# Two mixture-of-experts layers around two attentions: second weights resident in SBUF, one layer's weights parked in DRAM, unused tiles left out

## What is computed

```python
x = x + 0.5 * L0_ffn(norm(x))    # 24 experts, D_FF 512, top 2 of 24
x = x + L0_attn(norm(x))         # linear attention, 16 "heads", softplus features
x = x + 0.5 * L0_ffn(norm(x))
x = x + 0.5 * L1_ffn(norm(x))    # 8 experts, H 256, top 2 of 8, and a shared expert
x = x + L1_attn(norm(x))         # causal softmax attention with rotary embedding
x = x + 0.5 * L1_ffn(norm(x))
```

## Time and profile before

| | us |
|---|---|
| median of 3 runs | 1047.45 (1044.62 to 1049.02) |
| span of the profiled execution (first to last instruction) | 1043.2 |
| TensorE busy / weight loads, beside it | 905.4 / 789.0 |
| VectorE, ScalarE, GpSimd busy | 569.7, 484.6, 497.2 |
| data moved | 200.19 MB |

### The profile page before, as it was taken

How to read it: one execution, slowest core, us unless ns; L and a number is a source line. 1 busy time by engine, 2 the same in 40 slices (tenths; PEclk the granted TensorE clock), 3 DMA queues, 4 the chain that set the end, 5 groups by cost and what they waited for, 6 DMA issues and landing times.

```text
span 1043.2 us, 26677 instructions
## 1 busy us (share of the span) xinstructions
PE 905.4 (87%) x8696; PEld 789.0 (76%) x8696; DVE 569.7 (55%) x2226; ACT 484.6 (46%) x814; POOL 497.2 (48%) x519
## 2 busy tenths in 40 slices
PE   4757999998999799999999998996899999998670
PEld 2327899976889777899888898883688867888570
DVE  7897500066785065785058400588883888872112
ACT  3333544448634257734345444352528455654320
POOL 0551560271027571035372743577744657277655
PEclk9886999999999899999999999898999999999985
DMA  9765999973578783488895899944658456669982
GB/s 306 242 205 156 300 308 242 237 203 95 123 191 231 187 212 104 118 208 234 218 254 146 209 274 226 230 129 130 153 141 189 124 115 165 142 155 247 258 196 75
DMA packets 278655, 200.19 MB, mean 192 GB/s; under 512 B 146112, under 2 KB 233536, under 8 KB 278400
## 3 DMA queue, kind: packets, MB, share of 16 engines
q1 hardware_dynamic: 262144, 164.90, 63.1%
q0 software_dynamic: 16384, 33.59, 11.2%
HBM read 115.56 MB, written 55.57 MB: 164 GB/s over the span
## 4 chain that ended last, share of the span: by engine, by line
PE 58%; DVE 20%; DMA 8%; issue 5%; ACT 4%; POOL 4%; SPq 1%; DVEq 0%; POOLq 0%; ACTq 0%
PE bank L1425 20%; PE bank L1403 5%; PE bank L1405 5%; PE bank L1404 5%; DMA turned<-rows 4%; PE bank L1291 4%; POOL got L2123 3%; PE bank L1244 3%; DMA got<-y_l,slot_index 3%; PE bank L1263 2%; PE bank L1220 2%; PE bank L1253 2%; PE bank L1422 2%; DVE xn L1708 2%; PE bank L1301 2%
## 5 line engine op out<-in xcount | busy, mean ns | idle before, releaser
L1425 PE MATMUL bank<-second,hid 128*128 128x128 f32 x2560 | 369.7, 287 | 0.0
L2123 POOL DMA_INDIRECT got<-y_l,slot_index x256 | 244.7, 956 | 236.4 <-DMA y_l<-y 114.3
L1425 PEld LDWEIGHTS bank<-second,hid 128*128 128x128 f32 x2560 | 324.7, 195 | 4.7 <-issue 3.0
L2103 POOL DMA_INDIRECT rows<-rows_sent,slot_index x192 | 187.8, 978 | 282.2 <-issue 167.7
L1575 ACT ACTIVATE hid<-bank 128x512 f32<-128x512 f32 x320 | 189.7, 597 | 280.4 <-PE bank L1405 266.0
L1403 PE MATMUL bank<-turned,blocks_l 128*128 128x128 f16 x1280 | 239.7, 222 | 41.1 <-DMA turned<-rows 31.2
L1921 DVE SCALAR_TENSOR_TENSOR x_res<-got,share,x_res 128x128 f32<-128x128 f32 x256 | 77.4, 348 | 319.5 <-DMA got<-y_l,slot_index 312.9
L1405 PE MATMUL bank<-turned,blocks_l 128*128 128x128 f16 x1280 | 239.8, 223 | 0.0
L1404 PE MATMUL bank<-turned,blocks_l 128*128 128x128 f16 x1280 | 239.1, 222 | 0.0
L1403 PEld LDWEIGHTS bank<-turned,blocks_l 128*128 x1280 | 127.6, 100 | 55.4 <-issue 52.7
L1404 PEld LDWEIGHTS bank<-turned,blocks_l 128*128 x1280 | 127.1, 99 | 8.9 <-issue 5.9
(11 more groups left out here) (208 smaller groups left out, 1215.6 us busy)
## 6 DMA issues: line engine op xcount, KB each, us to landing
second<-in_w_dram SPq DMA_DIRECT2D x243, 256.0 KB, 5.3
y_l<-y SPq DMA_DIRECT2D x104, 256.0 KB
second<-in_w_dram SPq DMA_DIRECT2D x192, 128.0 KB
got<-y_l,slot_index POOLq DMA_INDIRECT x256
rows<-set SPq DMA_DIRECT2D x1, 3584.0 KB, 14.9
rows<-set SPq DMA_DIRECT2D x7, 512.0 KB, 6.4
rows<-rows_sent,slot_index POOLq DMA_INDIRECT x192
hid<-in_w_dram SPq DMA_DIRECT2D x9, 256.0 KB, 5.2
```

Source lines behind the costliest of these rows:

```text
L1425: m = t.do.matmul(out, hid[:, at], second[:, at], start=False, stop=(c == C - 1))
L2103: d = g.do.indirect_dma_start(rows_dram[s], at, rows[:, 2 * D * i:2 * D * i + 2 * D], None)
L2123: d = g.do.indirect_dma_start(got_mem[slot][:, col:col + D], None, y_dram[layer][s][layer.team(ev.i)], at)
```

## The change

- `w2` of all experts is loaded once, fp32, into `blocks` beside the halves of `w1` (a block is now `2 * hidden + 4` words). `bring` and its buffers, registers and DMAs go. `l2` reads the block at the tile's address.
- The 128 columns of each selector become one column, which a matmul reads with step 0 (`spread`); `select_cut`, `first_select` and their loads go.
- Room: layer 1's `blocks` are filled, stored to `blocks_dram` (`park`), used as two of the three sets of the linear attention, and loaded back (`unpark`) when all linear products are made. Round 2 has two sets of two buffers. Weights and tables of the causal attention are loaded into layer 0's `blocks` after its last experts (`load_late`, `load_last`).
- Row buffers: 6 in place of 8, taken for a batch before its norm and given back after its scatter. `hid`: 4 in place of 3. Raw buffers: 8 for layer 0, 4 for layer 1. Layer 0's routing has one scratch (in `route_wide`).
- `l2` is planned behind the third following `l1`, not the second. Layer 1's first matrices are split after layer 0's, and layer 0's experts no longer wait for them.
- Tiles beyond the bound are neither computed nor stored: 55 and 23.
- The planner's durations and the rank table change.

```diff
-        self.units = self.tiles // self.unit
+        self.bound, self.unit = bound, SEQ // hidden
+        self.units = -(-bound // self.unit)
-        self.block = hidden + P // 2
+        self.block = 2 * hidden + 4
+    def filled(self, unit):
+        return min(self.unit, self.bound - unit % self.units * self.unit)
...
-RAW_BUFFERS = 10
+GOT_BUFFERS, HID_BUFFERS, ROW_BUFFERS = 4, 4, 6
+RAW_BUFFERS = [HID_BUFFERS + GOT_BUFFERS, GOT_BUFFERS]
+FIRSTS_AHEAD = 3
+PARKED_SETS = (0, 1)
+MID_SETS, MID_BUFFERS = 2, 2
...
-        "scatter": [[(GP, 1.27 * TOP_K * tokens, 2.2)]], "gather": [[(GP, 1.27 * TOP_K * BT, 2.4)]], "add": [[(VE, 2.4, 0.1)]],
+        "scatter": [[(GP, 1.1 * TOP_K * tokens, 2.2)]], "gather": [[(GP, 1.1 * TOP_K * BT, 2.4)]], "add": [[(VE, 2.8, 0.1)]],
-        "bring": [[(SY, 0.45 * unit + 0.08, 0.0), (DMA, 0.9, 2.0)]],
+        "fetch": [[(SY, 1.3, 0.0), (DMA, 1.75, 2.0)]],
-        "l1": [[(PE, 0.75, 0.22), (SC, 0.62, 0.16)]], "l2": [[(PE, 1.04 if unit == 1 else 1.09, 0.22)]]
+        "l1": [[(PE, 0.68, 0.22), (SC, 0.58, 0.16)]], "l2": [[(PE, 1.03 if unit == 1 else 1.17, 0.22)]]
... # Plan.prepare: behind layer 0's loads and splits
+        yield Await(["halved"])
+        for n, ev in enumerate(later):
+            self.spawn(first(ev) if ev.kind.startswith("w1") else second(ev), (0, 2, len(parts) + n))
+        yield Await([split_of(ev) for ev in W1_PARTS[1]] + W2_PARTS[1])
+        yield from load("park")
+        for n in PARKED_SETS:
+            self.open_set(n)
+        yield from load("load_weights")
+        yield Await(["zeroed"])
+        self.open_set(START_SET)
+        yield Await(["linears"])
+        self.grow(self.mid_sets, MID_SETS, Ev("linears", 0, 0, 0))
+        yield from load("unpark")
... # Plan.gate, experts
+        yield Take(self.rows, [Ev("turn_g", s, p, b)], 1)
-            yield Await([("l1", s, p, min(unit + 2, units[-1]))])
+            yield Await([("l1", s, p, min(unit + FIRSTS_AHEAD, units[-1]))])
... # rank_on
-    rank = (rank[0] + EARLIER.get((engine, ev.kind), 0),) + rank[1:]
-    if engine == PE:
-        return (expert, ev.kind == "l1") + rank
-    return (not expert, False) + rank
+    shift = EARLIER.get((engine, ev.kind), FIRST if expert and engine != PE else 0)
+    rank = (rank[0] + shift,) + rank[1:]
+    return (expert, ev.kind == "l1") + rank if engine == PE else rank
... # layer1, layer2
-                for j in range(layer.unit):
+                for j in range(layer.filled(ev.i)):
-                    select = block_parts(block_for(ev, j), H)[2]
-                    t.do.matmul(out, select, bcol("b2_0" if layer is L0 else "b2_1"), start=True, stop=False)
-                    for c in range(C):
-                        at = slice(j * H + c * P, j * H + c * P + P)
-                        m = t.do.matmul(out, hid[:, at], second[:, at], start=False, stop=(c == C - 1))
+                    _, _, second, select = block_parts(block_for(ev, j), H)
+                    t.do.matmul(out, spread(select), bcol("b2_0" if layer is L0 else "b2_1"), start=True, stop=False)
+                    for c, at in enumerate(spans(C)):
+                        m = t.do.matmul(out, hid[:, j * H + c * P:j * H + c * P + P], second[:, at], start=False, stop=(c == C - 1))
... # SyncE
+            def park_blocks(ev):
+                y.wait_ge(*w1_low.after_all(w1_splits[1]))
+                y.wait_ge(second_loaded[1], 16 * SECOND_LOADS)
+                y.wait_ge(*selects_made.after(SELECTS))
+                y.do.dma_start(blocks_dram, blocks[L1][:, :]).then_inc(block_parked.sem, 16)
+            def bring_blocks(ev):
+                y.wait_ge(block_parked, 16)
+                for s, outs in enumerate(every_out):
+                    y.wait_ge(*attn_made[s].after_all(outs))
+                y.do.dma_start(blocks[L1][:, :], blocks_dram).then_inc(block_back.sem, 16)
+            def load_second(ev, layer, source):
+                some = slice(ev.i * layer.E // SECOND_LOADS, (ev.i + 1) * layer.E // SECOND_LOADS)
+                dst = blocks[layer].rearrange("p (e c) -> p e c", e=layer.E)[:, some, layer.H:2 * layer.H]
+                y.do.dma_start(dst, source[some].rearrange("e p h -> p e h")).then_inc(second_loaded[int(ev.kind[3:])].sem, 16)
-            def bring_second(ev, expert):
...
-                for j in range(layer.unit):
-                    dst = second_mem[slot][:, j * H:(j + 1) * H].unsqueeze(1)
-                    y.do.dma_start(dst, w2[:, bass.ds(expert[ev.i * layer.unit + j], 1)]).then_inc(second_landed[slot].sem, 16)
```

More of the change, by code:

```diff
@@ L73 @@
 L1 = Layer("l1", 8, 256, 2)
+assert all(l.teams == 1 or l.units * l.unit == l.tiles for l in (L0, L1))
 MAX_TILES = max(l.tiles * l.teams for l in (L0, L1))
@@ L285, in __init__ @@
         self.banks = Pool(8)
-        self.xn, self.xt, self.sets, self.got, self.norms = Pool(2), Pool(2), Pool(EARLY_SETS), Pool(4), Pool(2)
-        for held in (BIAS_SET, ZERO_SET):
-            self.sets.free.remove((held, None))
-        self.late_sets, self.raw = Pool(0), Pool(RAW_BUFFERS)
-        self.turned, self.second, self.hid, self.y = Pool(4), Pool(7), Pool(3), Pool(2)
-        self.tensor = Pool(1)
+        self.xn, self.xt, self.sets, self.got, self.norms = Pool(2), Pool(2), Pool(EARLY_SETS), Pool(GOT_BUFFERS), Pool(2)
+        self.sets.free = []
+        self.mid_sets, self.late_sets, self.raw = Pool(0), Pool(0), [Pool(n) for n in RAW_BUFFERS]
+        self.turned, self.hid, self.y, self.rows = Pool(4), Pool(HID_BUFFERS), Pool(2), Pool(ROW_BUFFERS)
+        self.tensor, self.scratch = Pool(1), Pool(1)
+        self.linears, self.routes = STREAMS * SB, STREAMS * sum(PARTS[p] for p in range(ROUNDS) if LAYER[p] is L0)
         self.now, self.count, self.events, self.done, self.waiting, self.kept = 0.0, 0, [], set(), [], STREAMS
@@ L466, in prepare @@
             self.spawn(load("load_x", 0, b), rank)
-        for kind in ("load_half", "load_bias", "load_cut"):
+        for kind in ("load_half", "load_bias"):
             self.spawn(load(kind), rank)
+        self.spawn(selects(), rank)
+        self.spawn(ready(), rank)
         yield Sleep(4.0)
-        parts = [part(n) for n in range(len(W1_PARTS))]
-        for n, steps in enumerate(parts):
-            self.spawn(steps, (0, 2, n))
+        parts, later = W1_PARTS[0] + W2_PARTS[0], W1_PARTS[1] + W2_PARTS[1]
+        for n, ev in enumerate(parts):
+            self.spawn(first(ev) if ev.kind.startswith("w1") else second(ev), (0, 2, n))
             if n == 3:
@@ L484, in prepare, with late @@
         self.spawn(self.zeros(), rank)
[L485 to L492 removed]
+        yield Await(["halved"])
[11 more added lines that the diff above has]
+        yield from load("unpark")
+    def late(self):
+        for kind in ("load_late", "load_last"):
+            yield from self.stage(kind, 0, 0, 0)
+            self.mark(kind)
     def zeros(self):
@@ L591, in linear, with out @@
         yield from self.stage("la_moved", s, p, b)
-        yield from self.stage("la_out", s, p, b, {PE: lambda: self.give(self.sets, user)})
+        def out():
+            self.linears -= 1
+            if self.linears:
+                self.give(self.sets, user)
+            else:
+                self.mark("linears")
+        yield from self.stage("la_out", s, p, b, {PE: out})
     def causal(self, s, p, b):
+        yield Await(["load_late", "load_last"])
         yield from self.normed("a", s, p, b)
@@ L642, in ranked @@
             if layer is L0:
-                self.give(self.sets, user)
+                self.routes -= 1
+                self.give(self.scratch, user)
+                if not self.routes:
+                    self.mark("routes")
         yield from turn("r_slot", {VE: ranked})
@@ L678, in experts @@
         rank, turn = (2 * p + s, 3, team), Ev("experts", s, p, team)
-        left = {g: per_group for g in layer.rows(team)}
+        left = {g: sum(unit // per_group == g for unit in units) for g in layer.rows(team)}
         def fetch(g):
@@ L1765, in route_top @@
                     v.wait_ge(const_loaded, 16)
-                    if layer is L0:
-                        before_set(v, ev, SB + q)
+                    old = plan.scratch.before[Ev("scratch", ev.s, ev.p, q)] if layer is L0 else None
+                    if old:
+                        v.wait_ge(*slots_ready[old.s].after(Ev("r_slot", *old[1:])))
+                    if layer is L1:
+                        for s, ready in enumerate(slots_ready):
+                            v.wait_ge(*ready.after_all([Ev("r_slot", s, p, part) for p in range(ROUNDS) if LAYER[p] is L0
+                                                        for part in range(PARTS[p])]))
                     if ev.p:
```

450 lines of the change are left out of this document (237 added, 213 removed).

## The result

The changed kernel takes 1035.34 us (median of 4 runs, 1034.44 to 1036.59), the kernel before 1048.05 on the same chip (4 runs, 1044.62 to 1049.02): ratio 0.9883, 95% interval 0.9839 to 0.9927. So it is faster by 12.7 us, under half of the 27 forecast. The profiled execution took 1034.46 us, with a span of 1033.1, 10.1 under that of before.

What follows compares the result with a forecast made beforehand. TensorE, working 905.4 of 1043.2 us, was taken as the bound, with holes mostly for `turned`. Terms -13.8 - 8 - 5 - 2 - 2 + 2 + 2 = -26.8 gave span 1016.4, with 4.25 over it 1020 us; range 994 to 1042.

Steps and rivals of the forecast that it cites:

- All of the tiles' time counts, -13.8: Experts of both layers: leaving out never-used tiles saves their full time, TensorE being nearly always busy around them; -13.8 us.
- TensorE does the same products from another address: Second products of the experts: reading resident second weights instead of loaded buffers costs TensorE nothing; 0 us.
- the mark, over 1.67 us a tile: First experts, layer 0: more than 1.67 us a tile would mean that selector or address cost something.
- Second weights resident, -8: Last stage of experts, 960 to 1014 us: fetches no longer stand behind weight loads in SyncE's queue; -8 us.
- Handovers, -5: Where one stream's experts end and the other's begin: flights of last scatter and transpose shrink, 1.7 us at each of three.
- The start, -2: Before the first expert matmul at 88.77 us: some VectorE splits of first weights come later; -2 us, ends -8 and +8.
- Late splits: Start: first matrices queue behind second weights by 31 us, TensorE starts 5 us late, +8 for -2; 1030 us, chance 0.10.
- Layer 1's splits, +2: Identity products for layer 1's first matrices, moved later: cost 0 in 71:89, all 5 us behind 95 us; +2 taken.
- Four `hid` buffers, -2: Experts' second product three units behind the first, with four buffers: waits for `hid` and `y`, 7.9 us, shrink by 2.
- parking 0: Layer 1's block goes out and comes back, 8 to 15 us each, covered by other work; 0, at worst +5 us.
- selectors 0: Selectors by `spread`: the same 416 matmuls with their weight loads hidden; 0 us, ends 0 and +41.
- A stale order, 1060 by chance 0.13: Planner sets scatters and gathers at 1.10 us, trace has 1.25 to 1.26, so TensorE's steps stand too early; 1060 us, chance 0.13.

Runs made afterwards that it cites:

- clear job: A job whose traces lack the pauses before instructions that wait for nothing; the result's job was one, and the kernel before took 1048.05 us there.
- g1: Kernel before, every engine's order kept, without the products of the never-used tiles: 0.9984 of the kernel before, 1047.9 us.
- paused jobs: Four of the five experiment jobs: every kernel took 12% longer, with pauses on TensorE, VectorE and ScalarE before instructions that wait for nothing.
- h3: Kernel after, orders kept, products of the last unit of each round (one tile) emitted twice: 1.0268 of the kernel before, 1201.5 us.
- h4: Kernel before, orders kept, without second-weight loads except each buffer's first, their waits and SyncE's register loads: 0.9931 of the kernel before, 1160.6 us.
- i1: Kernel before, orders kept, without second-weight loads (as h4) and without never-used tiles' products (as g1): 0.9863 of the kernel before, 1154.4 us.
- f1: Kernel after with every tile's second matrix read at one fixed address of the resident block: 1.0063 of the kernel before, 1181.0 us.
- h2: Kernel after with every tile's second matrix at one fixed address, repeated in another job: 1.0086 of the kernel before, 1181.3 us.
- i2: i1 with the second products' operands at register addresses again, from the tile's own resident block: 0.9986 of the kernel before, 1169.2 us.
- f3: Kernel before with second products reading their operand at a register address, a repeat of e3: 1.012 of the kernel before, 1189.2 us.
- e3: Kernel before, loads and waits kept, second products reading their operand at a register address from the resident block: 1.0154 of the kernel before, 1198.5 us.
- e1: Kernel after with every tile's second matrix at one fixed address, the first such run: 1.0081 of the kernel before, 1192.5 us.
- e2: Kernel after with the selector's weight load reading 128 neighbouring columns instead of one column 128 times: 1.0192 of the kernel before, 1202.6 us.
- g3: Kernel before with the planner's duration of a scatter or gather at 1.10 us in place of 1.27: 1.0441 of the kernel before, 1096.0 us.
- g4: Kernel after with the planner's duration of a scatter or gather at 1.27 us in place of 1.10: 1.0301 of the kernel before, 1079.7 us.
- f0: Kernel after, unchanged, as a mark beside its variants: 1.0171 of the kernel before, 1192.3 us.
- h1: Kernel after, unchanged, as a mark beside its variants in another job: 1.0208 of the kernel before, 1196.1 us.
- g2: Kernel after with three first products of a chunk and one second product taking turns on TensorE: 0.993 of the kernel before, 1041.5 us.
- job g: The experiment job in which g1, g2, g3 and g4 ran; the kernel before took 1048.7 us there.
- job h: The experiment job in which h1, h2, h3 and h4 ran; the kernel before took 1170.5 us there.

## Why the prediction came out where it did

- *All of the tiles' time counts, -13.8.* This step failed. It was read from a busy share of 98% in 95:194, but a never-used tile is the last of its round, and behind several rounds TensorE waits for rows. With the order kept it gave 1 us in a clear job (g1); in paused jobs 5 (h3) and 8 (h4 to i1).
- *"TensorE does the same products from another address", 0.* This failed too. The products are the same, the queue's work is not: 11 to 17 us in five comparisons within paused jobs (f1, h2, i2, f3, e3), 10 for e1 against e2. In the clear trace of after 5.8 us of spacing are shown to be theirs, and 7.6 may be or not. The forecast named the mark, over 1.67 us a tile, and 1.76 came; it gave the cause no price. The trace of before had one: the `FUSED_REGOPS` ahead of each first product, which I had not counted.
- *Second weights resident, -8.* Right in mechanism: 8 to 10 for the residence in all (h4). In the kernel after the waits of the last stage went from 13.7 to 7.8, and the 5.73 us at 654.55 went too. The forecast had misread these as a third handover; it was the same queue of SyncE.
- *Handovers, -5.* This failed as well. At the two true ones the flights shrank by 0.7 us at the first, not 1.7, and the waits grew from 8.2 to 14.2. The forecast let only flights change a handover. It is a lead of the experts over GpSimd's scatters, and those were held by VectorE's slots (7.58 us for 1.97). That the traffic itself does not slow TensorE in 95:194 stands; GpSimd's pitch stayed.
- *The start, -2.* First expert matmul at 86.16, 2.6 us earlier. "Late splits" did not come.
- *Layer 1's splits, +2.* They came in 95:194, up to 6.7 us busy and 4.4 by the distance of their starts: nearer the end of +5.
- *Four `hid` buffers, -2; parking 0; selectors 0.* `hid` and `y` waits were 7.9 and are 3.2 + 1.9; nothing waits for parked blocks at a handover; the selector is settled by e2.
- *A stale order, 1060 by chance 0.13.* An order can cost as much as it said (47 us in g3), but 1.10 against 1.25 is not the reason (g4). The result's own order fits.

The sum with measured sizes: tiles -1 to -8, residence -8 to -10, registers +11 to +17 lies between -7 and +8, and i2 shows nothing for the three in one run. Those sizes are from paused jobs but for g1's. If they hold in a clear one, the result's -12.7 is left to new orders, buffers and the start. In paused jobs that remainder is +22 to +27 (f0, h1, less i2), and there TensorE's waits for nothing are 110 and 97 us, in i2 80: the new orders are the ones that the pauses hit more. The remainder was not separated in a clear job: the forecast had 0 for it, and no run shows which of its parts it is. Nor was the price of the register addresses measured by pairs in a clear job, and if it is smaller there, the remainder is too. How the parts add up to 12.7 thus stays open. That the time came out within the stated range owes something to luck: two terms of the sum were worth less than said, one cost had been left out, and something that the forecast had at 0 made up for part of it.

The Trainium skill, page "Perfetto Trace Analysis", section "Sequencer Loop", says that a control instruction is executed by the sequencer itself, while engine instructions are pushed on. The trace agrees in so far as the `FUSED_REGOPS` stand in a row of the sequencer (`PEldq`), 46 ns each, and with their products come one in 0.124 us where the queue is not ahead.

No kernel here that computes the same was faster than the changed one in a clear job. In paused jobs the kernel before is.

## What to carry to other kernels

Busy share says what an engine does, not what its time is worth: price removed work at the wait that follows it. When data moves from a fixed buffer to a place chosen at run time, count the register operations that each product now needs against the time of the products between two waits. If an order is computed from a cost table, measure each part with the order frozen: here one number moved either kernel by over 40 us, three times the whole effect. And before a wait is put down to a cause, look whose tiles stand on both sides of it: one "handover" here was a queue.

## What was not expected of the hardware

- An operand at a new register address takes 0.124 us of TensorE's queue with its product; 1250 of them cost 10 to 17 us in paused jobs, 8 to 14 ns each, since most hide.
- An fp32 product takes 0.224 us among its like and 0.28 between fp16 ones (g2, 154.62 to 154.90).
- A job can put every kernel 12% higher, on a chip that ran without that in another, with 92 to 149 pauses on TensorE, 58 to 110 us in all, where clear jobs have 7 to 13 and 6 to 9 us (chip 1: job g 1048.7, job h 1170.5). What causes them, the runs don't show. They take more from the new orders, and the ranking changes: 0.988 becomes 1.017 to 1.021.
